# Attention of a graph-network block: products in four column groups of TensorE, row sums added up by GpSimd

## The reference, cut to what matters

```python
h = relu(layernorm(x))                     # eps 1e-5, no scale
q, k, v = h @ W_qkv                        # 4 heads of 32
attn = softmax(q k^T / sqrt(32) + mask)    # mask: -inf where adj == 0
x = x + attn @ v
h = relu(layernorm(x))
h = relu(adj @ (h @ Wg0 + bg0))
h = relu(adj @ (h @ Wg1 + bg1))
for p in 1..4:                             # LSTM over windows of p tokens
    h[last token of each window] = lstm_last(p, windows of h)
x = x + h
```

## Time and profile before

| | us |
|---|---|
| median of three runs | 537.26 (537.23 to 538.68) |
| the profiled execution | 531.79, its span 530.0 |
| iterations 4 to 15 of the pipeline | 17.1 each |
| busy in the span: TensorE, VectorE, ScalarE, GpSimd | 94%, 77%, 65%, 28% |

### The profile page before, as it was taken

One profiled execution on the slowest core, in us unless ns is written; L12 is line 12 of the kernel. 1 busy time (PEld: TensorE's weight loads), 2 busy tenths in 40 slices (PEclk: granted clock), 3 DMA queues, 4 the chain that ended last, 5 costly groups with the idle time before them and its releaser, 6 DMA issues.

```text
span 530.0 us, 9995 instructions
## 1 busy us (share of the span) xinstructions
PE 496.4 (94%) x3464; PEld 429.9 (81%) x3464; DVE 409.3 (77%) x929; ACT 343.1 (65%) x561; POOL 150.1 (28%) x167
## 2 busy tenths in 40 slices
PE   3787999999999999999998899999999999999994
PEld 2577888888888888888888787888999987888884
DVE  3856887788777977788665678888888879986875
ACT  2456766686667766686656776777776757665551
POOL 2434325442545335442101012111222122222211
PEclk9999999999999999999998999999999999999998
DMA  7332000000000000000000000000000000000225
GB/s 213 98 99 80 22 2 1 2 0 0 0 0 0 0 0 0 0 0 0 2 1 1 1 1 0 2 0 1 1 1 1 0 2 0 1 0 1 80 80 158
DMA packets 18778, 11.29 MB, mean 21 GB/s; under 512 B 662, under 2 KB 17724, under 8 KB 18748
## 3 DMA queue, kind: packets, MB, share of 16 engines
q1 hardware_dynamic: 17052, 10.03, 6.7%
q10 hardware_dynamic: 1696, 0.87, 0.6%
HBM read 6.70 MB, written 4.19 MB: 21 GB/s over the span
## 4 chain that ended last, share of the span: by engine, by line
PE 71%; DVE 14%; ACT 7%; issue 4%; DMA 2%; POOL 1%; DVEq 0%; ACTq 0%; SPq 0%; POOLq 0%
PE ps L894 25%; PE ps L830 10%; PE ps L739 7%; PE ps L750 6%; DVE S_hi L1208 3%; PE ps L843 3%; PE ps L771 3%; PE ps L787 3%; PE ps L848 2%; PE ps L936 2%; DVE arena L1195 2%; PE ps L761 2%; PE ps L804 2%; PE ps L802 2%; PE ps L803 2%
## 5 line engine op out<-in xcount | busy, mean ns | idle before, releaser
L599 ACT ACTIVATE arena<-ps,bias 128x512 f32<-128x512 f32 (+1 forms) x207 | 121.2, 625 | 45.4 <-PE ps L894 43.6
L563 ACT ACTIVATE arena<-ps 128x512 f32<-128x512 f32 (+1 forms) x112 | 77.6, 720 | 49.0 <-PE ps L750 42.3
L543 POOL TENSOR_TENSOR arena<-arena 128x512 f32<-128x512 f32 (+1 forms) x36 | 43.5, 1208 | 179.6 <-ACT arena L599 179.6
L894 PE MATMUL ps<-H_hi,W_hi 128*128 128x512 f32 (+2 forms) x207 | 75.6, 365 | 3.3 <-DVE S_lo L1210 2.2
L894 PE MATMUL ps<-H_lo,W_hi 128*128 128x512 f32 (+2 forms) x207 | 74.8, 362 | 0.0
L894 PE MATMUL ps<-H_hi,W_lo 128*128 128x512 f32 (+2 forms) x207 | 74.8, 361 | 0.0
L830 PEld LDWEIGHTS ps<-arena 128*128 128x128 f32 x512 | 64.1, 191 | 12.7 <-issue 8.5
L830 PE MATMUL ps<-arena 128*128 128x33 f32 x512 | 63.5, 269 | 3.6 <-ACT arena L563 2.0
L510 POOL TENSOR_TENSOR veps<-mv,eps 128x4 f32<-128x4 f32 x32 | 11.7, 365 | 183.9 <-DVE mv L1064 183.9
L520 POOL TENSOR_SCALAR arena<-X,mv,rstd 128x128 f32<-128x128 f32 x56 | 59.4, 1071 | 1.5
L739 PE MATMUL ps<-ident,arena 128*128 128x128 f32 x384 | 50.3, 279 | 7.7 <-POOL arena L520 2.7
(11 more groups left out here) (105 smaller groups left out, 981.6 us busy)
## 6 DMA issues: line engine op xcount, KB each, us to landing
X<-in_x_dram SPq DMA_DIRECT2D x16, 256.0 KB, 2.8
out_dram<-X SPq DMA_DIRECT2D x14, 256.0 KB, 2.4
out_dram<-X ACTq DMA_DIRECT2D x2, 256.0 KB, 3.9
arena<-in_L_gnn_W_dram ACTq DMA_DIRECT2D x1, 128.0 KB, 3.1
wg<-in_L_gnn_Wg_dram ACTq DMA_DIRECT2D x2, 64.0 KB, 2.3
bg_rows<-in_L_gnn_bg_dram SPq DMA_DIRECT2D x6, 0.5 KB
wv<-in_L_gnn_W_dram ACTq DMA_DIRECT2D x1, 64.0 KB, 3.1
adj_sb<-in_adj_dram SPq DMA_DIRECT2D x1, 64.0 KB, 3.3
```

What stands on the lines that cost most here:

```text
L543: g_.tensor_tensor(ig[:, it.buf, 0:w], sig_i[:, it.buf, 0:w], tanh_g[:, it.buf, 0:w], ALU.mult)\
L563: a_.activation(to, psum, func).then_inc(ready, 1)
L599: a_.activation(to[:, it.buf, 0:w], ps[:, 4 * it.par + j, 0:w], func, bias=bias[:, col:col + 1])\
L894: l = mm(o, wt, v, start=m == 0, stop=m == len(terms) - 1)
```

## The change

**TensorE.** `attend` is one piece for all four heads. The values (128 by 32) are now the weights, loaded into the column group of their head, and the transposed probabilities (128 columns) are streamed; the four heads of a batch use the four column groups and write to four quarters of the partitions of one bank. The result has features in the partitions, so that it must be copied to SBUF by ScalarE (`read_att`) and transposed back (`attended`, four transposes) after `scores`. The column of ones is gone. In the order of the engine, `graph_mix` now stands ahead of the key product, and both `graph_linear_1` and the key product stand ahead of the transposes of half 1.

**GpSimd.** `add_halves` adds the exponentials of a row by folding 128 to 64, 32 and 16, by halves of the heads. It waits for `xn2_ready`, the second norm of this iteration. VectorE reduces the 16 that are left.

**VectorE.** The product with the reciprocals and the addition to `X` are made one iteration later, after shift 0, for all heads at once (`add_attention`), with the moments of layer 2 behind them. `normalize` of layer 2 now stands ahead of shift 1. Epsilon is added here.

**ScalarE.** The relu of `hn2` moves up to behind `v`, `u1T` moves up to behind `hT`, and the copy of the first half of the probabilities comes after both. `read_att` stands behind the tanh.

```diff
@@ GpSimd
-            def rsqrt(layer, g, var, ve, done):
-                pool.wait_ge(var, g + 1)
-                g_.tensor_tensor(veps[:, layer, :], mv[:, layer, :, 1], eps[:], ALU.add).then_inc(ve, 1)
+            def rsqrt(layer, g, ve, done):
                 pool.wait_ge(ve, g + 1)
                 g_.tensor_tensor(rstd[:, layer, :], veps[:, layer, :], minus_half[:], ALU.pow).then_inc(done, 1)
...
+            def add_halves(s, half):
+                n = s.k * 2 - 1 + half
+                part = slice(2 * half * GB, 2 * (half + 1) * GB)
+                pv = prob.rearrange("p (c n) -> p c n", n=N)[:, part, :]
+                pool.wait_ge(exp_ready, n)
+                g_.tensor_tensor(by_64, pv[:, :, 0:N // 2], pv[:, :, N // 2:N], ALU.add).then_inc(by_64_ready, 1)
+                pool.wait_ge(by_64_ready, n)
+                g_.tensor_tensor(by_32, by_64[:, :, 0:N // 4], by_64[:, :, N // 4:N // 2], ALU.add)\
+                    .then_inc(by_32_ready, 1)
+                pool.wait_ge(by_32_ready, n)
+                if s.back:
+                    pool.wait_ge(sums_row, s.k - 1)
+                g_.tensor_tensor(by_16[:, part, :], by_32[:, :, 0:N // 8], by_32[:, :, N // 8:N // 4], ALU.add)\
+                    .then_inc(by_16_ready, 1)
...
             def iteration(s):
                 if s.back:
-                    rsqrt(1, s.k - 2, var2, veps2, rstd2)
+                    rsqrt(1, s.k - 2, veps2, rstd2)
+                if s.mid:
+                    if s.back:
+                        pool.wait_ge(xn2_ready, s.k - 1)
+                    add_halves(s, 0)
+                    add_halves(s, 1)
@@ ScalarE
+            def read_att(s):
+                read(att, psO, att_done, s.k, att_read)
...
-                if s.mid:
-                    read_probT(s, 0)
+                read(hn2, hn2, xn2_ready, k - 1, hn2_ready, ACT.Relu)
                 if s.next1:
                     read_hT(psX[s.back], k + 2, 1 - s.par)
+                read(u1T[:], psA, u1_done, k - 1, u1T_ready)
+                if s.mid:
+                    read_probT(s, 0)
                 if s.finish:
                     if s.after:
                         act.wait_ge(first_h, k - 3)
                     first_gate(k - 3, 0, act_i, 0, 0.5)
-                read(hn2, hn2, xn2_ready, k - 1, hn2_ready, ACT.Relu)
                 if s.mid:
                     exp(s, 1)
...
-                read(u1T[:], psA, u1_done, k - 1, u1T_ready)
...
+                read_att(s)
                 read(u2T[:], psA, u2_done, k - 1, u2T_ready)
@@ TensorE
-            def attend(s, half):
-                def part(b):
-                    if b == 0:
-                        pe.wait_ge(probT_ready, s.k * 2 - 1 + half)
-                    for h in (2 * half, 2 * half + 1):
-                        o = b * 2 + h % 2
-                        l = mm(psO[:, half, o * (HD + 1):(o + 1) * (HD + 1)], probT[:, h, b * N:(b + 1) * N],
-                               v_sb[:, 1 - s.par, b, h, :], start=True, stop=True)
...
+            def attend(s):
+                pe.wait_ge(probT_ready, s.k * 2)
+                for b in range(GB):
+                    at_ = slice(b * N, (b + 1) * N)
+                    for h in range(HEADS):
+                        l = mm(psO[h * HD:(h + 1) * HD, at_], v_sb[:, 1 - s.par, b, h, :], probT[:, h, at_],
+                               start=True, stop=True)
+                l.then_inc(att_done, 1)
+
+            def attended(s):
+                pe.wait_ge(att_read, s.k)
+                transposed(psR, batches(att)).then_inc(attT_done, 1)
...
                     pe.wait_ge(xn_ready, k + 2)
-                    pe.wait_ge(att_read, 2 * k - 2)
+                    pe.wait_ge(x2_ready, k - 1)
                     transposed(psX[s.back], xn).then_inc(xnT_done, 1)
                 first_gate(s, 0, 0)
-                if s.mid:
-                    if s.front:
-                        pe.wait_ge(q_ready, k + 1)
-                    interleave([], attend(s, 0))
-                if s.front:
-                    if s.next1:
-                        pe.wait_ge(hT_hi_ready, k + 2)
-                    pe.wait_ge(att_read, 2 * k - 2)
-                    interleave([], project(s, psK, D, k_done))
                 pe.wait_ge(hn2_ready, k - 1)
                 if s.front:
                     pe.wait_ge(v_ready, k + 1)
                 interleave([], graph_mix(hn2, u1_done))
-                if s.mid:
-                    transpose_prob(s, 1)
+                if s.front:
+                    if s.next1:
+                        pe.wait_ge(hT_hi_ready, k + 2)
+                    pe.wait_ge(x2_ready, k - 1)
+                    interleave([], project(s, psK, D, k_done))
                 pe.wait_ge(u1T_ready, k - 1)
...
                 graph_linear_1().then_inc(z1_done, 1)
+                if s.mid:
+                    transpose_prob(s, 1)
                 first_gate(s, 1, 2)
-                masks = []
                 if s.front:
+                    pe.wait_ge(probT_ready, k * 2 - 1)
                     put_mask((0, 1))
                     pe.wait_ge(probT_ready, k * 2)
+                    put_mask((2, 3))
+                    pe.wait_ge(q_ready, k + 1)
                     pe.wait_ge(k_ready, k + 1)
-                    masks = [lambda h=h: put_mask((h,)) for h in (2, 3)]
-                interleave(attend(s, 1), masks)
+                attend(s)
                 if s.front:
                     scores()
+                attended(s)
@@ VectorE
                 l.then_inc(var, 1)
+                dve.wait_ge(var, g + 1)
+                v_.tensor_scalar(veps[:, layer, :], mv[:, layer, :, 1], LN_EPS, None, ALU.add).then_inc(ve, 1)
...
-            def over_sums(s, half):
...
+            def over_sums(s):
+                dve.wait_ge(by_16_ready, s.k * 2)
+                v_.tensor_reduce(row_sums[:], by_16, AX_X, ALU.add).then_inc(sums_row, 1)
+                dve.wait_ge(sums_row, s.k)
+                v_.reciprocal(rec[:], row_sums[:]).then_inc(rec_ready, 1)
+
+            def add_attention(k):
+                dve.wait_ge(rec_ready, k - 1)
+                dve.wait_ge(attT_done, k - 1)
+                by_head = lambda T: T.rearrange("p (b h d) -> p h b d", b=GB, h=HEADS)
+                v_.tensor_tensor(by_head(att_n), by_head(psR),
+                                 rec[:].rearrange("p (h b) -> p h b", h=HEADS).unsqueeze(3)
+                                 .to_broadcast([P, HEADS, GB, HD]), ALU.mult).then_inc(att_scaled, 1)
+                dve.wait_ge(att_scaled, k - 1)
+                xg = X[:, ds(k * GB - 2 * GB, GB), :]
+                v_.tensor_tensor(xg, xg, batches(att_n), ALU.add).then_inc(x2_ready, 1)
+                dve.wait_ge(x2_ready, k - 1)
+                moments(1, k - 2, stats2, var2, veps2)
...
                 if s.mid:
                     shift(s, 0)
                 if s.back:
-                    dve.wait_ge(x2_ready, 2 * k - 2)
-                    moments(1, k - 2, stats2, var2)
+                    add_attention(k)
...
                 if s.finish:
                     output_lo(k - 3)
+                if s.back:
+                    normalize(1, k - 2, xn2, rstd2, xn2_ready)
                 if s.mid:
                     shift(s, 1)
...
-                if s.back:
-                    normalize(1, k - 2, xn2, rstd2, xn2_ready)
...
-                    moments(0, k + 2, stats1, var1)
-                if s.mid:
-                    over_sums(s, 0)
+                    moments(0, k + 2, stats1, var1, veps1)
...
                 if s.mid:
-                    over_sums(s, 1)
+                    over_sums(s)
```

More of the change, by code:

```diff
@@ L264, in gnn_block @@
         qT, kT, att = take(GT), take(GT), take(GT)
-        v_sb = take(V).rearrange("p (s b h d) -> p s b h d", s=2, b=GB, h=HEADS)
+        v_sb = take(2 * GT).rearrange("p (s b h d) -> p s b h d", s=2, b=GB, h=HEADS)
         prob = take(HEADS * GT)
@@ L268, in gnn_block @@
         probT = take(HEADS * GT).rearrange("p (h n) -> p h n", h=HEADS)
+        by_64 = take(GT).rearrange("p (c n) -> p c n", n=N // 2)
         at[0] = attention_end = 16 * GT
@@ L274, in gnn_block @@
         act_i, act_g, act_o, u1T = take(GT), take(GT), take(GT), take(GT)
+        att_n = take(GT)
+        by_32 = take(GT // 2).rearrange("p (c n) -> p c n", n=N // 4)
+        by_16 = take(GT // 2).rearrange("p (c n) -> p c n", n=N // 8)
         assert at[0] <= ARENA
@@ L305, in gnn_block @@
         psX = {True: psK, False: psB}
-        psO = ps[:, 4:6, :]
+        psO, psR = ps[:, 4, :], ps[:, 5, :]
         def psW(m):
@@ L362, in gnn_block @@
         att_done = sem("att_done")
+        by_64_ready = sem("by_64_ready")
+        by_32_ready = sem("by_32_ready")
+        by_16_ready = sem("by_16_ready")
+        sums_row = sem("sums_row")
         rec_ready = sem("rec_ready")
+        att_scaled = sem("att_scaled")
         att_read = sem("att_read")
+        attT_done = sem("attT_done")
```

(22 more changed lines are left out.)

53 lines of the change are left out of this document (20 added, 33 removed).

## The result

The changed kernel takes 551.57 us, median of four runs (550.77 to 552.12), against 537.25 for the kernel before on the same chip (533.99 to 538.68): a ratio of 1.0302, 95% interval 1.0251 to 1.0352. It is slower by 3%, inside the range and on the side that was forecast. The profiled execution took 550.77, span 549.0; before it was 531.79 and 530.0, so profile against profile it is +19.0 where +18.8 was forecast.

A forecast was written before the change was run, and what follows sets the result against it. TensorE bounds the kernel before; after, the ring of 18.1 us against 17.1 does. Twelve intervals +12, two before +2.5 and +1.6, iteration 16 +3.2, fill -0.6: +18.8 on 537.3 gives 556 us, range 545 to 576.

The forecast's parts named there:

- TensorE stops setting the pace: TensorE's list falls to 15.7 us per iteration, and it stands for 3 us of each, no longer the bound.
- The 0.1 for one more change of tile shape: TensorE, eight products behind the scores: 1.09 us against 0.81 elsewhere, so up to 0.3 per change, taken as 0.1.
- Step 1: VectorE's shift 0, from its release by the scores: 2.39 us.
- Step 2: VectorE, new behind shift 0: a product and an addition of 128 by 512, 0.68 each with a hop, 1.46 us.
- Steps 3 to 7: Moments and epsilon 1.59, GpSimd's power 1.41, normalize 1.14, relu of hn2 0.68, graph_mix to ScalarE's copy 1.20 us.
- The 0.35 for contention: GpSimd's power, starting just as VectorE's L1160 does, takes over the 0.35 us that epsilon's addition lost beside it.
- Step 8: ScalarE runs u1T, first probabilities' copy and gate 0 ahead of exp 1: 2.1 us; exp 1 waits 1.5 for this order.
- Steps 9 and 10: Exp 1, transposes and their copy 3.31 us; then masks 0.45, attention 1.20, scores to VectorE's release 1.20, together 2.85.
- The row sums: Rival: GpSimd's additions take over 4.5 us per half, so VectorE waits before shift 0; 571 us at 5.5; chance 0.05.
- The clock: Rival: TensorE's waits bring half-clock stretches, about 1 us each in the ring, one per iteration: 571 to 580; chance 0.10.
- the ring: Loop from one set of scores over VectorE's shifts, ScalarE's exponentials and the transposes to the next: 17.0 us before, 18.1 after.
- Full serial groups: Rival: attention's column groups on TensorE do not overlap, 3.55 us for 1.10, 2.45 more per iteration: 594; chance 0.08.

The follow-up runs named there:

- the doubled product: TensorE's value product issued twice per iteration, nobody reading the extra: on the kernel before 540.6 us (ratio 1.0131), on the changed kernel 552.95 us (1.0359).
- the three kernels whose ring was lengthened to 19.6 us or more: Changed kernel with GpSimd's additions not waiting for the second norm (585.89 us), attention loops swapped (575.5), or second normalize behind shift 1 (587.41).
- the four moves alone: Changed kernel with first probabilities' copy before hn2, gate 0 behind exp 1, first_h_part behind shift 1, attention's copy before tanh: 527.57 us.
- the one with 20.45: Changed kernel with normalize of the second norm moved back behind shift 1 on VectorE: 587.41 us, ratio 1.1011.

## Why the prediction was right, point by point

- **TensorE stops setting the pace.** Right: 15.65 busy for 15.7 forecast, waiting 2.6 us of each iteration for 3, and the doubled product costs 7 us before and 1.4 after. The 0.1 for one more change of tile shape came from an unlike pair: the eight instructions at 136.42 stream 33 columns, the eight behind the scores 128. Like beside like, `graph_mix` takes 0.91 us to the next start behind the scores and 0.89 where no change of shape is ahead of it, so 1.09 against 0.81 shows no price of a change of shape. What the trace after has is 0.21 us from the last start of the attention (144.29) to the first of the scores (144.50), where inside the attention one start follows another by 0.03.
- **Step 1**, shift 0: 2.40 (2.39 forecast). **Step 2** was mis-sized: 1.71 for 1.46. The addition waits 0.18 for its own engine's product and the moments 0.16 for the addition, as the brackets at 130.74 and 131.59 say; the walk had one hop for both.
- **Steps 3 to 7**: 1.58, 1.46, 1.15, 0.68, 1.20 for 1.59, 1.41, 1.14, 0.68, 1.20. The 0.35 for contention, a choice, is shown by moving first_h_part.
- **Step 8**: 1.96 for 2.1, and exp 1 stands 1.49 after its shift for the 1.5 forecast. Shown by moving the copy and the gate.
- **Steps 9 and 10**: from exp 1 to the attention 3.87 for 3.76, the attention 1.01 with its change of tile shape for 1.20, the scores to VectorE's release 1.24 for 1.20. The attention was taken at the scores' rate, 1.10 for 32, plus 0.1; it took 1.01 with the change.
- **The sum** of the steps is 18.26 for 18.1, so twelve intervals gave 13.5 for 12. Before them it was +2.7 for +3.5 (fill -1.2 for -0.6, then +2.7 for +2.5 and +1.2 for +1.6), the last iteration +2.5 for +3.2, in which the kernel before had a stretch at half clock in its profile that the forecast did not take off, the rest +0.3 for nothing. The errors cancel to 19.0 for 18.8, so that this nearness is luck in part; the terms as written add up to 18.7.
- **The step from the profiled run to the median** is the one that failed: "a step costs the same in both" set 18.8 on a median of 537.3, 5.5 above its profile, which later runs show at a lower clock only. The changed kernel's runs, at 0.991 and more, lie within 1.4 us of their profile, and 556 became 551.6. Set on 534.2, the median of more runs, the same sum gives 553. The 0.3% that a measurement was said to tell from no change is too small by that: the later runs of the kernel before spread over 1.2%.
- **Rivals.** The row sums were not late, and the additions' wait is what keeps normalize at 1.11. The groups overlap. The clock kept its upper level in the steady loop of the change; it fell in the three kernels whose ring was lengthened to 19.6 us or more, in many of their iterations. The price of a stretch in the ring, about 1 us in the prediction, was 0.2 to 0.8 for 3.41 us at half clock. Full serial groups cost 1.38 and not 2.45.

## What to carry to other kernels

Where one engine is full, walk the second-longest ring too, from one instruction through every engine back to itself: 1.3 us taken from TensorE bought nothing, because the ring behind it was about as long, and the change lengthened that one, by 0.9 us through the later copy alone. (That the ring before was 17.0 us long is the prediction's walk; no run measured it.) Then look at the order of each engine inside the ring: what stands ahead of the ring's instruction and is not due (here a copy and a gate ahead of exp 1) costs its whole time, and moving it, together with one VectorE instruction that stood beside GpSimd's power, gave a kernel 1.1% faster than before with the same results. Take the base of a forecast from runs whose clock is that of the profile.

## What was unexpected of the hardware

- Beside additions of GpSimd, VectorE's normalize went from 1.11 to 2.89 us, and ended 0.34 after the last of the three additions. The other way round, a power of 4 elements per partition on GpSimd took 1.42 instead of 1.03 beside a two-input instruction of VectorE.
- 32 PE instructions (16 products) with weights of 32 columns and 128 columns streamed take 1.01 us in turn over four column groups and 2.39 one group after another: 0.032 and 0.075 each.
- The granted clock of 0.50 came in stretches of 3.4 or 6.8 us, and once of 10.2 in each of two kernels. Runs of the same kernel with a mean clock of 0.979 to 0.982 took 3 to 6 us longer than those at 0.992 and more, of before and of the four moves alike. In profiles with an iteration of 16.6 to 18.3 us it did not occur in the steady loop; in the one with 20.45 it occurred once in each of ten iterations in a row.
